# Softmax sums of a cross attention by a block of ones on TensorE, and an output bias added four batches at a time on GpSimd

## What is computed

```python
q = (query @ Wq.T + bq); k = (key @ Wk.T + bk); v = (value @ Wv.T + bv)   # 16 heads of 8
scores = jnp.einsum('bhtd,bhsd->bhts', q, k) * scale
scores = scores + attn_mask[None, None, :, :]
scores = scores + spatial_bias + directional_bias
probs = jax.nn.softmax(scores, axis=-1)
out = jnp.einsum('bhts,bhsd->bhtd', probs, v)
return out @ Wo.T + bo
...
x = x + _L0_attn_ref(_layernorm(x, axis=-1), ...)
x = x + _L0_xattn_ref(_layernorm(x, axis=-1), ctx_1024, ctx_1024, ...)
x = x + _L0_ffn_ref(_layernorm(x, axis=-1), ...)
```

## Time and profile before

| | us |
|---|---|
| median of three runs | 622.98 (621.36 to 623.25) |
| the profiled execution | 620.23 |
| its span, first to last instruction | 618.5 |
| PE busy, share | 511.4, 83% |
| DVE busy, share | 497.3, 80% |
| ACT busy, share | 432.0, 70% |
| POOL busy, share | 369.5, 60% |

### The profile page before, as it was taken

The page is one execution under the profiler, slowest core; times in us unless marked ns, Lnnn a source line. Parts: engine busy times, 40 slices in busy tenths (PEclk is TensorE's granted clock), DMA queues, the critical chain, the costliest instruction groups (busy, mean ns, idle before and its releaser), DMA issues. The chain is left out here.

```text
span 618.5 us, 15993 instructions
## 1 busy us (share of the span) xinstructions
PE 511.4 (83%) x4272; PEld 380.2 (61%) x4272; DVE 497.3 (80%) x2009; ACT 432.0 (70%) x1545; POOL 369.5 (60%) x392
## 2 busy tenths in 40 slices
PE   4689999999996768777777777777766899999986
PEld 3466777777774445555555555555545678788874
DVE  2677888888876269999999999999986788898872
ACT  2668787887872269999999999999984333333321
POOL 6236554555534778888888888888932233444430
PEclk9899999999998669999999999999997799999999
DMA  6910000000000447888888888888700000000000
GB/s 159 239 21 1 1 2 0 0 0 0 2 1 2 72 98 130 144 144 146 144 145 143 149 146 145 147 147 147 119 2 2 0 18 19 17 17 17 19 18 17
DMA packets 84422, 42.37 MB, mean 69 GB/s; under 512 B 4378, under 2 KB 84132, under 8 KB 84388
## 3 DMA queue, kind: packets, MB, share of 16 engines
q1 hardware_dynamic: 83234, 41.63, 36.6%
q10 hardware_dynamic: 1154, 0.33, 0.2%
HBM read 39.86 MB, written 2.10 MB: 68 GB/s over the span
## 5 line engine op out<-in xcount | busy, mean ns | idle before, releaser
L960 ACT ACTIVATE c_P<-c_P,c_min 128x128 f32<-128x128 f32 x512 | 204.7, 461 | 0.0
L1129 POOL TENSOR_TENSOR c_bias<-c_fside,c_cm 128x2048 f32<-128x2048 f32 x32 | 145.4, 4545 | 2.7 <-DVE c_cm L1046 2.7
L960 ACT ACTIVATION_READ_ACCUMULATOR c_P<-c_P,c_min 128x1 f32 x512 | 132.8, 260 | 0.0
L1021 DVE CUSTOM_DVE_ANT_0 c_P<-banks,c_bias 128x128 f32<-128x128 f32 x512 | 117.0, 285 | 7.9 <-issue 3.6
L916 PE MATMUL banks<-ident,c_P 128*128 128x128 f32 x512 | 80.7, 286 | 8.1 <-ACT c_P L960 6.4
L916 PEld LDWEIGHTS banks<-ident,c_P 128*128 128x128 f32 x512 | 57.5, 144 | 22.6 <-ACT c_P L960 12.9
L1056 DVE COPY shared<-banks 128x512 f32<-128x512 f32 x96 | 65.9, 686 | 2.8 <-PE banks L916 2.8
L1471 POOL TENSOR_TENSOR xs<-shared,xs 128x512 fp32r<-128x512 f32 x8 | 10.7, 1343 | 85.7 <-ACT xs L1303 85.7
L1236 PE MATMUL banks<-um,lb_s 128*128 128x512 f32 x192 | 55.7, 405 | 2.7 <-ACT shared L1293 1.9
L1293 ACT ACTIVATE shared<-banks,bi_col 128x512 f32<-128x512 f32 x32 | 22.0, 688 | 38.9 <-PE banks L1236 38.9
L903 PE MATMUL banks<-x_wT,shared 128*128 128x128 f32 x64 | 15.2, 321 | 40.1 <-DVE shared L1051 40.1
(11 more groups left out here) (197 smaller groups left out, 1340.9 us busy)
## 6 DMA issues: line engine op xcount, KB each, us to landing
c_fside<-in_fside_Bx16xSxS_dram SPq DMA_DIRECT2D x64, 512.0 KB, 7.2
c_ctx<-in_ctx_dram SPq DMA_DIRECT2D x32, 64.0 KB, 5.3
out_dram<-shared SPq DMA_DIRECT2D x8, 256.0 KB, 2.3
X<-in_x_dram SPq DMA_DIRECT2D x3, 512.0 KB, 5.4
kmask_sb<-in_mask_BxS_bf_dram SPq DMA_DIRECT2D x1, 512.0 KB, 7.2
X<-in_x_dram SPq DMA_DIRECT2D x2, 128.0 KB, 3.5
c_P<-in_L_ffn_wi_dram SPq DMA_DIRECT2D x1, 256.0 KB
c_P<-in_L_ffn_lora_B_dram SPq DMA_DIRECT2D x1, 256.0 KB
```

Of the source, the lines that this page charges most:

```text
L960: last = nc.scalar.activation(P[:, par, h, :], P[:, par, h, :], ACT.Exp, bias=mn[:, par, h:h + 1], scale=-1.0, accum_out=rsx[:, par, h:h + 1])
L1021: last = nc.vector.tensor_tensor_reduce(out=P[:, o, h, :], in0=bank(SCORE_BANKS[i])[:, 128 * j:128 * j + 128], in1=fm[:, o, h, :], scale=- ...
L1129: nc.gpsimd.tensor_tensor(fm[:, q, :, :], fs[:, q, :, :], bc(cm[:], XH), ALU.add).then_inc(C["fm"], 1)
```

## The change

The row sums no longer come from ScalarE's accumulator. A block `head_ones` with ones in the places where `vp` has the eight values of a head is multiplied with the same turned weights, so that the sums of each head stand in PSUM beside the mixed values, already in the layout in which they are needed. ScalarE inverts them as exp(-ln(sum)), and VectorE's `outputs` multiplies by that. VectorE's two instructions for the reciprocals, TensorE's transposition of them and ScalarE's copy go. The turned inputs are copied in one instruction. The output bias is added by GpSimd as before for the first four batches, and for the others in the feed-forward, one group of four batches in each of the ticks -1 to 5.

```diff
@@ -267,8 +267,9 @@
                                   lb_in.rearrange("p c k -> p (c k)").rearrange("p (e c r) -> p c e r", e=E, c=FC)).then_inc(s_lb, 1)
 
         def setup_constants(pool):
-            fill(pool, (ones, 1.0), (twos, 2.0), (vp, 0.0), (in_head, 1.0), (before, 1.0))
+            fill(pool, (ones, 1.0), (twos, 2.0), (vp, 0.0), (head_ones, 0.0), (in_head, 1.0), (before, 1.0))
             keep(pool, before, ALU.is_gt, 0, [[1, E], [-1, E]], 0)
+            pool_step(pool, nc.gpsimd.memset(head_ones[:].rearrange("p (j w) -> p j w", j=XG)[:, :, 0:XD], 1.0))
             in_block(pool, in_head, XH, XD)
             pool.sem_inc(s_const, 1)
...
-        rsx = sb("c_sum", [128, 2, XH])
+        head_ones = sb("c_ones", [128, VPAD])
...
-            def reciprocals_turned():
-                need(pe, C["rx"], n)
-                need(pe, C["oT"], n - 1)
-                nc.tensor.transpose(bank(7)[:, 0:128], rx[:].rearrange("p h d -> p (h d)"), ident[:]).then_inc(C["Rp"], 1)
-
             def queries_keys():
                 need(pe, C["T"], n + 3)
-                nc.tensor.matmul(bank(0)[:, 0:128], x_wT[:, 0, :], xT2[:], start=True, stop=True)
-                nc.tensor.matmul(bank(0)[:, 128:256], x_wT[:, 1, :], cT[:, q, :], start=True, stop=True).then_inc(C["qkp"], 1)
+                for w in range(2):
+                    last = nc.tensor.matmul(bank(0)[:, 128 * w:128 * w + 128], x_wT[:, w, :], xcT[:, q, w, :], start=True, stop=True)
+                last.then_inc(C["qkp"], 1)
...
+                need(pe, C["oT"], n - 1)
+                for w in range(2):
+                    for j in range(XG):
+                        for i in range(NI):
+                            block = vp[:, o, VPAD * i + 32 * j:VPAD * i + 32 * j + 32] if w == 0 else head_ones[:, 32 * j:32 * j + 32]
+                            last = nc.tensor.matmul(bank(7)[32 * i:32 * i + 32, 128 * w:128 * w + 128], block,
+                                                    PTs[:, o, i, 128 * j:128 * j + 128], start=(j == 0), stop=(j == XG - 1))
                 last.then_inc(C["pv"], 1)
...
-                    last = nc.scalar.activation(P[:, par, h, :], P[:, par, h, :], ACT.Exp, bias=mn[:, par, h:h + 1], scale=-1.0,
-                                                accum_out=rsx[:, par, h:h + 1])
+                    last = nc.scalar.activation(P[:, par, h, :], P[:, par, h, :], ACT.Exp, bias=mn[:, par, h:h + 1], scale=-1.0)
                 last.then_inc(C["ex"], 1)
...
-                nc.scalar.copy(xT2[:], bank(0)[:, 0:128])
-                nc.scalar.copy(cT[:, q, :], bank(0)[:, 128:256]).then_inc(C["T"], 1)
+                nc.scalar.copy(xcT[:, q, :, :].rearrange("p w t -> p (w t)"), bank(0)[:, 0:256]).then_inc(C["T"], 1)
...
+            def denominators():
+                need(act, C["pv"], n)
+                need(act, C["rc"], n - 1)
+                nc.scalar.activation(log_den[:], bank(7)[:, 128:256], ACT.Ln).then_inc(C["ln"], 1)
+                need(act, C["ln"], n)
                 need(act, C["oT"], n - 1)
-                nc.scalar.copy(RT[:], bank(7)[:, 0:128]).then_inc(C["RT"], 1)
+                nc.scalar.activation(inv_den[:], log_den[:], ACT.Exp, scale=-1.0).then_inc(C["rc"], 1)
...
+            if finish:
+                denominators()
...
+                need(dve, C["rc"], n)
                 need(dve, C["yv"], n + 1)
-                nc.vector.tensor_tensor(oTs[:], bank(7)[:, 0:128], RT[:], ALU.mult).then_inc(C["oT"], 1)
+                nc.vector.tensor_tensor(oTs[:], bank(7)[:, 0:128], inv_den[:], ALU.mult).then_inc(C["oT"], 1)
...
-            def reciprocals():
-                need(dve, C["ex"], 4 * n + 4)
-                nc.vector.reciprocal(rc[:], rsx[:, q, :]).then_inc(C["rc"], 1)
-
-            def reciprocals_spread():
-                need(dve, C["rc"], n + 1)
-                need(dve, C["Rp"], n)
-                nc.vector.tensor_copy(rx[:], inner(rc[:], XD)).then_inc(C["rx"], 1)
...
-                need(dve, C["xbias"], n)
+                need(dve, C["xbias"], min(n, GROUP) if isinstance(n, int) else GROUP)
...
+            if project and isinstance(n, int) and n + 2 < GROUP:
+                output_bias()
             if project:
-                output_bias()
...
+                need(dve, M["biased"], t + 1)
...
+            def stream_bias():
+
+                need(pool, C["x2"], min(GROUP * (t + 3), B) if isinstance(t, int) else B)
+                x3 = X[:, bass.ds(GROUP * (t + 2), GROUP), :] if not isinstance(t, int) else X[:, GROUP * (t + 2):GROUP * (t + 3), :]
+                nc.gpsimd.tensor_tensor(x3, x3, bc(x_bias[:], GROUP), ALU.add).then_inc(M["biased"], 1)
...
+            if add:
+                stream_bias()
...
-            tick(t // 2, t % 2, *(0 <= t + k < GROUPS for k in (1, 0, -1)))
+            tick(t // 2, t % 2, *(0 <= t + k < GROUPS for k in (2, 1, 0, -1)))
```

More of the change, by code:

```diff
@@ L904, in outputs_values @@
                 if scores:
[L905 removed]
+                    last = nc.tensor.matmul(bank(0)[:, 128:256], xcT[:, o, 1, :], x_wT[:, 2, :], start=True, stop=True)
                 last.then_inc(C["yv"], 1)
@@ L1198, in decoder, with f_tensor @@
             "eq2", "sum", "rank", "top", "et", "num", "den", "rden", "vs", "hot1", "hot", "hp", "um", "i1", "r1", "i2", "h",
-            "y", "out", "bias", "added",
+            "y", "out", "bias", "added", "biased",
             "x_high", "x_low", "u_high", "u_low")}
         s_out = [sem(f"stored{i}") for i in range(2)]
-        def f_tensor(pe, m, q, norm, route, expert):
+        def f_tensor(pe, m, q, add, norm, route, expert):
             t = 2 * m + q
```

38 lines of the change are left out of this document (10 added, 28 removed).

## The result

| | before | after |
|---|---|---|
| median, us | 623.12 (621.36 to 623.81, 4 runs) | 636.61 (634.55 to 636.95, 4 runs) |
| profiled execution: span, us | 618.5 | 634.5 |
| `cm` to `cm`, mean of 27 periods, us | 7.66 | 7.74 |
| last `cm` (step 29) to last copy of `PTs` (step 31), us | 23.2 | 27.4 |
| tick 0, tick 1, us | 14.7, 17.0 | 15.9, 21.0 |

The ratio is 1.0216, 95% interval 1.0188 to 1.0244: slower by 13.5 us, where 13.7 was forecast (636.7 us). A second series of the changed kernel gave 637.31 us, ratio 1.0225 (1.0199 to 1.0252), and the two intervals overlap. The total came out as predicted; its parts did not, and the table already shows where. A tick is counted from one start of the turned normalisation on TensorE (`x_turned`) to the next.

A forecast was written before the change was run, and what follows sets the result against it. ScalarE and VectorE were near the limit, VectorE's own programme setting 7.66 us a step. The terms 5.9 - 0.4 + 1.0 + 1.2 + 6.0 = +13.7 us, on the median 622.98, gave 636.7 us; range of 8 in 10: 626 to 643.

The forecast's parts named there:

- The 28 periods: Cross attention, step 1 to step 29: each step grows from 7.66 to 7.87 us, 28 x 0.21 = +5.9 us.
- what would show it: Signs: `cm` to `cm` near 7.87 us, ScalarE idle before Ln, TensorE and VectorE waits, exponentials 0.29 us apart, ticks 17.2 us.
- the ring: Cross attention: ScalarE waits for TensorE's mixing, TensorE for ScalarE's exponentials; one round, 7.87 us, is the period's lower bound.
- The 0.33 for Ln: Cross attention, ScalarE: Ln of 128 columns to Exp, estimated between rows of 0.42, 0.47 and 0.36 us.
- twice the mixing: Cross attention, TensorE: mixing and the added ones block, 1.06 us each, 2.12 us together.
- The spacing of the exponentials: Cross attention, ScalarE: without the accumulator, exponentials start 0.29 us apart instead of 0.38.
- The rival of 0.25 us: Cross attention: exponentials follow at 0.25 us, the step takes 7.39 us, the time is 623.2 us; chance 0.12.
- The transition: Tail of the cross attention: doubled mixing costs more than its earlier start saves, +1.0 us, bounds -0.4 and +1.8.
- Tick -1: Feed-forward: GpSimd's bias there is covered, since GpSimd has nothing after it; no cost.
- Ticks 0 and 2 to 5: Feed-forward: GpSimd's bias delays `u_low`, and VectorE's `um` waits for it without cover, +1.2 us a tick.
- Tick 1: Feed-forward: same pattern as the following ticks, `um` waits for `u_low` behind the bias, +1.2 us.
- GpSimd's relief "brings nothing": Cross attention: some 0.5 us per step taken from GpSimd saves nothing, since GpSimd was not the bound there.

The follow-up runs named there:

- acc_kept: The changed kernel with accumulators put back on all 16 exponentials of a step, their sums unused: 670.22 us, ratio 1.0764.
- no_ones: The changed kernel without the 16 matmuls of ones, an Exp with scale 0 in place of Ln, so dividing by a constant: 622.66 us, ratio 1.0006.
- ln_later: The changed kernel with Ln and Exp of the sums moved behind the exponentials of quarter 3 on ScalarE: 623.38 us, ratio 1.0012.
- cross_only: The changed kernel with the output bias added per batch in the cross attention, as before: 627.08 us, ratio 1.0066.
- bias_last: The changed kernel with GpSimd's output bias moved behind `u_low` and the gated bias of the same tick: 634.80 us, ratio 1.020.
- best: The changed kernel with Ln and Exp behind quarter 3's exponentials, and the output bias last in the tick, waiting for VectorE's `xn3`: 613.83 us, ratio 0.9867.

## Why the prediction was right, and where its terms were not

The forecast was 636.7 us, and 636.6 came. On the profiled spans +16.0 us came, +13.7 was summed. Term by term:

**The 28 periods: predicted +5.9, measured +2.2** in the 27 of them between first and last `cm` (209.0 against 206.8 us), or 0.08 us each where 0.21 was predicted. The mechanism was right: every sign in "what would show it" appeared, `acc_kept` moved the step by the amount that the ring gives, and `no_ones` and `ln_later`, which shorten the ring below VectorE's programme, took it down to that. The sizes were 0.13 us off in 7.87. By the rows above the ring is Ln to Exp 0.30 (predicted 0.36), 0.22, eight exponentials 2.34 (2.32), copy 0.47 (0.46), quarter 1 and hand-over 1.32 (1.31), turning 0.39, queries and keys 0.65 (0.64), mixing to Ln 2.02 (2.12 + 0.05): 7.71 us for this step, 7.74 in the mean. (TensorE's starts are here those of its weight loads, 357.67, 358.06 and 358.71, as in the prediction.) The 0.33 for Ln does not lie between the rows that it names, whose least is 0.36; Ln took 0.28. The term that failed is "twice the mixing": 1.06 was the distance to the next work of another kind, and the second block of 32 follows the first after 0.90. An error of 2% in the ring is 60% of the difference of 0.21 us, since that is a small difference of two large numbers; the range had to be wide for that reason. Step 0, predicted at -0.4, got 0.5 us shorter (from its `cm` to the next, 8.83 to 8.32).

**The spacing of the exponentials: predicted 0.29, measured (2.43 - 0.39)/7 = 0.29.** The rival of 0.25 us is out. The estimate from the Trainium skill (ScalarE: Activation LUTs, section "What ACT_TABLE_LOAD costs"), 0.29 us apart, agrees with this row. The Identity pair, which also has a bias column, still follows at 0.25; the exponentials do not. `acc_kept` gives the accumulator's price: (8.86 - 7.74)/12 = 0.093 us each.

**The transition: predicted +1.0, bounds -0.4 and +1.8; measured +4.2.** Three things were missed. Tick -1 was called covered "since GpSimd has nothing after it": that looked at GpSimd's queue and not at VectorE beside it, which was blocked for 0.96 us. The mixing at the lower clock was seen as a bound, in which the whole doubling falls, but the value was taken near the middle. And a bound of this part was taken as the bound of the stretch: `cross_only`, with no bias in tick -1 and the upper clock at that mixing, is 1.4 us longer there, and what makes up this part was not taken apart.

**Ticks 0 and 2 to 5: predicted 1.2 each; measured +1.2 and, in the mean of four, +1.14.** Right in size and in mechanism for the place where the change puts the bias: `um` waits for `u_low`. For tick 0 this holds for the first execution only; in the second it took 17.3 us, +2.6. `bias_last` shows that the queue was not the only price at hand, and that removing the wait alone would have brought 0.2 us.

**Tick 1: predicted +1.2, measured +3.95.** By the clock rows above the rest goes with the clock, which falls once more behind the wait; no run separates the two. It came again in the second profile.

**Ones and Ln alone, predicted +6.5, cost 4.1 us by the ratio (4.4 by the medians); the bias alone, predicted +7.2, 8.7 (6.6).** The total agreed because an overestimate of 3.7 us in the steps stood against underestimates of 3.2 in the transition and 2.8 in tick 1 (and 0.2 too much in ticks 2 to 5). The sum of the profiled spans was 2.3 us short, and the median of the kernel before lay further above its profiled execution (2.9 us) than that of the changed one does (0.35 us, 636.61 against 636.26). The 0.1 us between forecast and result is therefore luck; the sign and the size to a few us are not.

**GpSimd's relief "brings nothing"**: right for the changed kernel (`cross_only`, 7.76 us a step), wrong as a general statement (0.16 us a step once the ring is open, most of it VectorE's mask blocked beside GpSimd).

## What to carry to other kernels

When a result moves from one engine to another, write down the ring of engines that it closes, and add up one round start to start. If it exceeds the period, look for work on the waiting engine that does not depend on the result and put it in front of the wait: here one reordering on ScalarE gave back 13 us with no arithmetic changed. A slot on GpSimd was free here only where VectorE, beside it, had one of its inputs in PSUM; find that slot in VectorE's timeline, not in GpSimd's.

## What the runs showed of the hardware that was not expected

- Five VectorE instructions that read only SBUF stood still until a GpSimd addition or subtraction of 128x128 or 128x512 ahead of them was through, whatever their own size: 0.19 became 1.29 us, 0.42 became 1.52, 0.16 became 1.26, four of `xn3` went from 1.11 to 2.07 us, the mask `cm` from 0.29 to 0.58. The kernel before has it as well and pays for it in every tick: its second comparison takes 1.67 us beside `x_low`, where the same instruction took 0.70 in tick 3 of `best`. Beside GpSimd's root of 128x4, listed at 1.46 us, nothing was lengthened (a product of 128x32 in `best`, at 519.04, took 0.19).
- One wait of TensorE of about 3 us just after its clock had risen (to 2.4 GHz, near 487 us) was followed by some 10 us at 1.2 GHz, though TensorE was busy from 492 on; tick 1 took 20.8 and 21.0 us in two executions, against 16.0 at the upper level in `best`. Which part of that wait matters, and whether it is the wait at all, was not tried.
- Two mixings in a row took 0.90 us to the second's start and 1.12 from there to ScalarE's Ln, 0.15 us less than twice 1.06 and a hand-over.
